# A one-core graph attention layer: the part up to the end of the first group laid out anew

## The reference

```python
h = jnp.maximum(_layernorm(x, axis=-1), 0.0)        # x: 4096 x 256
# the attention layer, on h:
h = h @ W.T
src = h @ a1
dst = h @ a2
e = jax.nn.leaky_relu(src[:, None] + dst[None, :], negative_slope=0.2)
e = jnp.where(adj == 0, -9e15, e)                   # adj: 4096 x 4096 int32
out = x + jax.nn.softmax(e, axis=1) @ h
```

## Time and profile before

| | us |
|---|---|
| median of 3 runs | 390.15 |
| lowest, highest | 389.91, 390.94 |
| profiled execution, its own time | 390.14 |
| its span | 388.6 |
| TensorE busy | 380.4 (98%) |
| VectorE busy | 366.8 (94%) |
| ScalarE busy | 196.7 (51%) |
| GpSimd busy | 43.6 (11%) |

### The profile page before, as it was taken

How to read it: one execution, slowest core, us unless ns; L and a number is a source line. 1 busy time by engine, 2 the same in 40 slices (tenths; PEclk the granted TensorE clock), 3 DMA queues, 4 the chain that set the end, 5 groups by cost and what they waited for, 6 DMA issues and landing times.

```text
span 388.6 us, 9271 instructions
## 1 busy us (share of the span) xinstructions
PE 380.4 (98%) x3368; PEld 330.2 (85%) x3368; DVE 366.8 (94%) x478; ACT 196.7 (51%) x282; POOL 43.6 (11%) x73
## 2 busy tenths in 40 slices
PE   6999899999999999999999999999999999999996
PEld 6788588888888888888888888888888888888885
DVE  4999999999999999999999799999988999999965
ACT  5899956553345643444445543444445543444430
POOL 3898002000000001110000001200000011100000
PEclk9999999999999999999999999999999999999999
DMA  8920176776559567776666567766665567766403
GB/s 255 371 79 3 43 246 222 267 232 231 171 175 292 182 216 218 244 232 220 221 221 205 183 216 231 240 221 220 215 205 179 167 217 239 229 231 215 162 2 108
DMA packets 26112, 77.95 MB, mean 201 GB/s; under 512 B 2916, under 2 KB 8552, under 8 KB 26088
## 3 DMA queue, kind: packets, MB, share of 16 engines
q1 hardware_dynamic: 24528, 74.20, 59.0%
q0 software_dynamic: 1280, 3.16, 2.2%
q10 hardware_dynamic: 280, 0.26, 0.3%
HBM read 73.40 MB, written 4.21 MB: 200 GB/s over the span
## 4 chain that ended last, share of the span: by engine, by line
PE 89%; DVE 4%; POOL 2%; ACT 1%; DMA 1%; issue 1%; ACTq 0%; DVEq 0%; POOLq 0%
PE ps L1280 87%; DMA w_f<-w_t 1%; POOL hn_sb L392 1%; DVE v_sb L767 1%; DVE hnt_lo L754 1%; PE ps L1218 1%; PE ps L1230 0%; ACT c_row L495 0%; DVE rows_sb L1130 0%; PE ps L1237 0%; PE ps L1234 0%; DVE hn_sb L762 0%; ACT hn_sb L474 0%; POOL v_sb L397 0%; ACT h_sb L467 0%
## 5 line engine op out<-in xcount | busy, mean ns | idle before, releaser
L1280 PE MATMUL ps<-v_sb,p_hi 128*128 (+2 forms) x2048 | 253.5, 272 | 1.4 <-ACT p_hi L505 1.4
L515 ACT ACTIVATE p_hi<-p_sb,gp 128x1024 f16<-128x1024 f32 x126 | 144.4, 1149 | 167.7 <-DVE p_sb L795 138.8
L1280 PEld LDWEIGHTS ps<-v_sb,p_hi 128*128 128x128 f16 x2048 | 198.3, 97 | 30.0 <-ACT p_hi L505 1.5
L802 DVE SCALAR_TENSOR_TENSOR p_lo<-p_sb,gp,p_hi 128x1024 f16<-128x1024 f32 x126 | 160.5, 1277 | 9.0 <-ACT p_hi L515 8.8
L795 DVE SCALAR_TENSOR_TENSOR p_sb<-c_row,gp,adj_sb 128x1024 f32<-128x1024 uint32 (+1 forms) x126 | 160.2, 1276 | 0.0
L1280 PE MATMUL ps<-v_sb,p_lo 128*128 (+1 forms) x1024 | 142.4, 273 | 0.0
L1280 PEld LDWEIGHTS ps<-v_sb,p_lo 128*128 128x128 f16 x1024 | 99.6, 97 | 13.5 <-DVE p_lo L788 0.3
L451 POOL DMA_DIRECT2D out<-rows_sb x24 | 13.0, 544 | 260.7 <-DVE rows_sb L1097 260.7
L392 POOL TENSOR_SCALAR hn_sb<-x_sb,moments,rstd 128x256 f32<-128x256 f32 x17 | 21.1, 1247 | 8.0 <-DVE rstd L744 8.0
L1218 PE MATMUL ps<-ident,hn_sb 128*128 128x128 f32 x64 | 12.8, 291 | 2.0 <-ACT hn_sb L474 1.5
L467 ACT ACTIVATE h_sb<-ps 128x258 f32<-128x258 f32 x32 | 12.2, 383 | 3.0 <-PE ps L1237 2.7
(11 more groups left out here) (96 smaller groups left out, 112.1 us busy)
## 6 DMA issues: line engine op xcount, KB each, us to landing
adj_sb<-adj_t SPq DMA_DIRECT2D x128, 512.0 KB, 4.8
x_sb<-x SPq DMA_DIRECT2D x7, 512.0 KB, 8.9
out<-rows_sb POOLq DMA_DIRECT2D x24, 128.0 KB, 4.5
c_row<-c_flat SPq DMA_DIRECT2D x3, 512.0 KB, 5.1
out<-rows_sb SPq DMA_DIRECT2D x8, 128.0 KB, 1.7
x_sb<-x SPq DMA_DIRECT2D x2, 256.0 KB, 4.3
w_nat<-w SPq DMA_DIRECT2D x1, 256.0 KB, 2.9
w_f<-w_t ACTq DMA_DIRECT2D x1, 256.0 KB, 5.2
```

Source lines behind the costliest of these rows:

```text
L515: nc.scalar.activation(p_hi[:, u % R, :], p_sb[:, u % R, :], ACT.Copy, scale=p_scale[:, bass.ds(t, 1)])\
L802: nc.vector.scalar_tensor_tensor(out=p_lo[:, u % R, :], in0=p_sb[:, u % R, :], scalar=p_scale[:, bass.ds(t, 1)], in1=p_hi[:, u % R, :], op ...
L1280: return nc.tensor.matmul(ps[:, k, 0:width], part[:, u % R, k * P:(k + 1) * P], v_sb[:, bass.ds(t, 1), v, 0:width], start=start, stop=stop ...
```

## The change

1. `w_f` is loaded on SyncE's queue, behind the first chunk of `x`, and no longer on ScalarE's.
2. Tiles 4 to 7 are one batch of statistics: nine batches in place of ten. VectorE normalises no tile any more (before 20, 25, 30); ScalarE has 14 (before 12), GpSimd 18 (before 17). `value_hi` falls to other engines for some tiles.
3. All turned tiles lie in one ring of RT = 8; `first_hi` and `first_lo` are gone.
4. `spread_s` with its twelve products and the copies `w1_hi`, `w1_lo` are gone. In their place `turn_s` turns the column s of each of tiles 0 to 7 from `h_sb`, broadcast to 128 columns: eight fp32 transposes of 128 columns, all behind `spread_d`. The exponent's scale for it is another column of `exp_scale`.
5. `spread_d` reads the last four tiles from the ring, one projection earlier; the turn of `d_up` is a step of its own, `turn_d`, into bank 1.
6. TensorE's order is a written list; `project` is cut in three (`project_hi`, `project_w_lo`, `project_lo`). One more product of `ones` stands behind the four of `w_nat`.
7. The lists of the other three engines are written anew. Before `d_up` VectorE has `value_lo` of tiles 0 to 9 (before 0 to 12), before the first `weights_part` 0 to 11 (before 0 to 14); GpSimd's five scale instructions stand behind its last `normalise`. In the first group VectorE waits for `p_lo_ready` of four tiles back ahead of every `edge_weights` from tile 4 on, before only ahead of some.

```diff
-    TURN_AHEAD = ((0, 1), (3, 2), (SOON, 3))
-    SPREAD_AFTER = {9: (0, 0), 11: (0, 1), 30: (1, 0), 31: (1, 1)}
+    BUSY_START, BUSY_SUMS, BUSY_SPLIT = 5, 1, 1
-    BATCHES = [(a, a + 2) for a in range(0, 2 * XB, 2)] + [(a, a + XB) for a in range(2 * XB, T, XB)]
+    BATCHES = [(0, 2), (2, 4), (4, 8), (8, 12), (12, 16), (16, 20), (20, 24), (24, 28), (28, 32)]
+    RT = 8
...
             for m, (t0, t1) in enumerate(X_CHUNKS):
                 sp.dma_start(x_sb[:, t0:t1, :], x_v[:, t0:t1, :]).then_inc(x_loaded[m], 16)
+                if m == 0:
+                    sp.dma_start(w_f[:, :, 0:F], w_tv).then_inc(w_t_loaded, 16)
...
-            act.dma_start(w_f[:, :, 0:F], w_tv).then_inc(w_t_loaded, 16)
...
-            def spread_s(m, c):
-
-                part = slice(m * CW, (m + 1) * CW)
-                last_chunk = c == KC - 1
-                nc.tensor.matmul(ps[:, bank_s + m, :], w1_hi[:, c, :], first_hi[:, c, part], start=(c == 0), stop=False)
-                nc.tensor.matmul(ps[:, bank_s + m, :], w1_lo[:, c, :], first_hi[:, c, part], start=False, stop=False)
-                last = nc.tensor.matmul(ps[:, bank_s + m, :], w1_hi[:, c, :], first_lo[:, c, part],
-                                        start=False, stop=last_chunk)
+            def turn_s(t):
+                pe.wait_ge(*kept(t))
+                last = nc.tensor.transpose(ps[:, bank_s + t // CT, t % CT * P:(t % CT + 1) * P],
+                                           h_sb[:, t, F:F + 1].to_broadcast([P, P]), ident[:])
+                if t % CT == CT - 1:
+                    last.then_inc(s_spread, 1)
...
+            def turn_d():
+                pe.wait_ge(d_part_ready, 1)
+                pe.wait_ge(hnt_lo_ready, LAST_IN_BANK_D_TURNED + 1)
+                nc.tensor.transpose(ps[:, banks_t[-1], 0:P], d_up[:, 0:1].to_broadcast([P, P]), ident[:]).then_inc(d_turned, 1)
```

More of the change, by code:

```diff
@@ L543, in _ @@
             split_hn_hi(2)
+            normalise(4)
+            split_hn_hi(3)
             keep_h(1)
+            keep_h(2)
+            split_hn_hi(4)
+            normalise(6)
             std_of(3)
[L546 to L550, removed]
             split_hn_hi(5)
-            std_of(4)
             keep_h(3)
@@ new lines, in _ @@
+            project_hi(0)
+            project_w_lo(0)
+            project_lo(0)
+            project_hi(1)
+            turn(2)
+            project_w_lo(1)
+            project_lo(1)
+            turn(3)
+            project_hi(2)
+            project_w_lo(2)
+            project_lo(2)
+            turn(4)
+            turn(5)
+            project_hi(3)
+            project_w_lo(3)
+            project_lo(3)
+            project_hi(4)
+            project_w_lo(4)
+            turn(6)
+            project_lo(4)
@@ new lines, in _ @@
+            turn(7)
+            project_hi(5)
+            project_w_lo(5)
+            project_lo(5)
+            project_hi(6)
+            project_w_lo(6)
+            project_lo(6)
+            turn(8)
+            project_hi(7)
+            project_w_lo(7)
+            turn(9)
+            project_lo(7)
+            turn(10)
+            project_hi(8)
+            project_w_lo(8)
+            project_lo(8)
+            project_hi(9)
+            project_w_lo(9)
+            project_lo(9)
@@ new lines, in _ @@
+            turn(11)
+            project_hi(10)
+            project_w_lo(10)
+            project_lo(10)
+            turn(12)
+            turn(13)
+            project_hi(11)
+            project_w_lo(11)
+            project_lo(11)
+            project_hi(12)
+            project_w_lo(12)
+            turn(14)
+            project_lo(12)
+            turn(15)
+            project_hi(13)
+            project_w_lo(13)
+            project_lo(13)
+            project_hi(14)
+            project_w_lo(14)
@@ new lines, in _ @@
+            project_lo(14)
+            turn(16)
+            project_hi(15)
+            project_w_lo(15)
+            project_lo(15)
+            turn(17)
+            project_hi(16)
+            project_w_lo(16)
+            project_lo(16)
+            turn(18)
+            project_hi(17)
+            turn(19)
+            project_w_lo(17)
+            project_lo(17)
+            project_hi(18)
+            project_w_lo(18)
+            project_lo(18)
+            turn(20)
+            project_hi(19)
@@ new lines, in _ @@
+            project_hi(24)
+            turn(26)
+            project_w_lo(24)
+            turn(27)
+            project_lo(24)
+            project_hi(25)
+            project_w_lo(25)
+            turn(28)
+            project_lo(25)
+            turn(29)
+            project_hi(26)
+            turn(30)
+            project_w_lo(26)
+            project_lo(26)
+            turn(31)
+            project_hi(27)
+            project_w_lo(27)
+            project_lo(27)
+            spread_d()
```

507 lines of the change are left out of this document (269 added, 238 removed).

## The result

The changed kernel takes 387.69 us (median of 4 runs, 387.32 to 388.21), the kernel before 390.24 (389.91 to 390.94, 4 runs). The ratio is 0.9936, with a 95% interval of 0.9922 to 0.9951: 2.5 us faster. The forecast was 386.9 within 385.4 to 389.1. The profiled execution took 388.21 with a span of 386.5, the longest of the four.

The account below looks back on a forecast made before the run. TensorE's unbroken 336.22 us of products was taken to bound the kernel, gaining only by starting earlier, behind a front bound by no one engine. 390.14 - 3.3 (front) + 0 + 0.1 (first group) = 386.9 us, range 385.4 to 389.1.

Parts of the forecast that it names:

- D: Start of the products for d (`spread_d`), where the front was cut: forecast at 36.4, 3.3 us earlier than 39.72.
- The start: Before turn 0: `w_f` lands sooner, so `w_hi` at 6.5 and turn 0 at 7.75, 0.5 us earlier; bounds 0 and 0.8.
- The low clock: TensorE from turn 0 on: 3.3 us at 1.2 GHz and not 2.4, counted as 1.65 us lost.
- TensorE's 34.9: The front: TensorE reaches D at 34.9 with no waits, from 7.75 + 25.5 of work + 1.65 for the clock.
- The waits: The front: D taken as VectorE's no-wait 35.5 plus half of its 1.6 us of waits; TensorE had 2.3 before.
- From D to the first group: Between D and the long piece of products: first product at D + 5.6, net 0, bounds -0.4 and +0.5.
- The first group: VectorE's three more `value_lo` there take 1.0 of 1.16 us of cover, leaving 0.15; cost 0.1, up to 0.5.
- all waits stay: Rival for the front: VectorE's and TensorE's waits of before remain, D 37.2, 387.7 us; chance 0.23 shared with rival 3.
- ScalarE's added `normalise` are waited out: Rival for the front: TensorE waits 6.6 us in all for them, D 41.5, time 392.0 us; chance 0.04.
- The collision on the ports: Front: each of ten `value_lo` waits half a GpSimd `normalise`, 6 us on VectorE, time 392.0 us; chance 0.01.
- rival 3: First group: VectorE at least 1 us later than counted, TensorE waits at the last tile, 387.9 us; chance 0.23, shared.
- rival 4: Front runs as planned, waits under 0.5 and full clock sooner: D 35.0 to 35.4, 385.5 to 385.9 us; chance 0.15.

Follow-up runs that it names:

- b_wt_sp: The kernel before with only the load of `w_f` moved to SyncE's queue behind the first chunk of `x`: 390.19 us against 389.97 in its session.
- a_wt_act: The changed kernel with the load of `w_f` back on ScalarE's queue: 387.48 us, ratio 0.9934 to the kernel before.
- a_group3: The changed kernel with three more 256-column subtractions, read by nobody, on VectorE in the first group: 388.35 us, ratio 0.9951 to the kernel before.
- b_turn_s: The kernel before with the twelve wide products for s and GpSimd's two copies replaced by eight turns of kept columns: 390.47 us against 390.12.

## Why the prediction was right, and where it was off

The sum was 390.14 - 3.3 at D + 0.1 behind it. The profile has -2.60 at D and +0.67 behind it. The median of 387.69 would stand for a D of 36.6 (an estimate: less the 351.05 behind D). So the number for D was close, by terms that were off in both directions, and 0.6 behind D was missing.

**The start.** `w_hi` 6.52 for 6.5, turn 0 7.79 for 7.75: right in this profile. Over the ten with this order of loads turn 0 came between 7.73 and 8.64, so it is also luck. The sum let the 0.5 us count in full; `b_wt_sp` and `a_wt_act` show that the part is worth nothing in the median.

**The low clock.** This term was mis-sized: 1.65 us, as if the 3.3 us from turn 0 on were fixed. In the profile it was 6.2 us at half speed, 3.1 lost. It is not fixed: the same front had 3.3 to 6.2 us. With 1.5 more, TensorE's 34.9 becomes 36.4, and D was 37.12, with waits of 0.7. The step that failed is taking one execution's moment as the program's.

**The waits.** I took VectorE's 35.5 and half of its waits for D = 36.4. The order was wrong: in the changed kernel the chain is TensorE alone up to D, with waits of 0.7 for the 2.3 before, and at the earliest full clock of this front (11.2) D was 35.77, again with TensorE's 34.9 and such waits. That VectorE's sum gave nearly the same number is luck; no run shows VectorE at its 35.5. GpSimd's last `normalise` ended at 35.4 and not near 33, still ahead of the turn of tile 31; it had waited for `rstd` for 3.4 us in all, not 2, and lost 0.47 us in that last one (1.69 for 1.22).

**From D to the first group.** Net 0 was forecast. The fifth tile (its first products at 53.94, before 56.39) stands 16.82 behind D, before 16.67: 0.15 lost. The first product came at D + 6.03, 0.4 later than I put it, since ScalarE waited 0.30 for the turns of s.

**The first group.** A cover of 0.15 was forecast, and a distance of 0.16 was there: from the fifth tile to the last TensorE took 71.53 us in both kernels, so nothing was lost, for a forecast of 0.1. But `a_group3` shows that the 0.16 is no slack. The view of waits has one of 0.2 for L790 on a weight load in this group, which did not hold up the products.

**The turn to the second group.** At the last tile of the first group the gain is 2.45; at the end of the last product 2.18 (380.95 for 383.13). The 0.27 between was lost right behind the first group, where the sum had no term. ScalarE copies the finished rows and TensorE's next sixteen products need those banks. Before:

```profile
129.05 2.29 ACT L696 ACTIVATE rows_sb<-ps 128x257 f32<-128x257 f32 x8
130.57 1.93 PE L1280 MATMUL ps<-v_sb,p_hi 128*128 128x257 f16 x16
132.34 1.04 PE L1280 MATMUL ps<-v_sb,p_lo 128*128 128x257 f16 x8
```

and after:

```profile
127.60 2.29 ACT L691 ACTIVATE rows_sb<-ps 128x257 f32<-128x257 f32 x8
128.12 2.21 PE L1409 MATMUL ps<-v_sb,p_hi 128*128 128x257 f16 x16
129.38 0.11 PEld L1409 LDWEIGHTS ps<-v_sb,p_hi 128*128 128x128 f16 x2 [0.16 <-ACT rows_sb L691]
130.17 1.04 PE L1409 MATMUL ps<-v_sb,p_lo 128*128 128x257 f16 x8
```

The sixteen products take 2.05 for 1.77, and the copies begin 2.13 behind the first product of the last tile, before 1.13. The changed kernel's waits have a row for it that the kernel before has not:

```profile
PEld ps L1409 <- ACT rows_sb L691: 0.8, 5, 0.2
```

VectorE's edge weights for the next group start 0.25 ahead of the last tile's first product (125.22), before 1.24 (126.68), and ScalarE's `p_hi` and copies follow them. So the us of cover that VectorE gave up in the first group is the us by which the copies come later. This is a reading of the rows; it was not tested. The last 0.2 of the 0.67 stand behind the last product and were not located.

**The rivals.** That all waits stay (387.7) gave the right number by the wrong way: TensorE's waits went from 2.3 to 0.7, and the clock took their place. That ScalarE's added `normalise` are waited out did not happen: in the front TensorE waited 0.37 and 0.41, both ahead of projection 0. The collision on the ports did not happen as priced either: two `value_lo` took 0.74 us at the start of that `normalise` of 1.69 and a third 0.41 at its end, so GpSimd lost 0.47 in all beside its neighbours, and VectorE nothing. The first group did not become VectorE's (rival 3), but with nothing to spare. A D of 35.0 to 35.4 (rival 4) stands in no profile.

```profile
33.62 0.74 DVE L755 TENSOR_TENSOR v_sb<-h_sb,v_sb 128x256 f16<-128x256 f32 x2
```

By the rule of the Trainium skill (SBUF — State Buffer, "Who interferes with whom") one of the two is blocked for the other's whole instruction. The trace does not bear that out: VectorE was not held for GpSimd's 1.22 us, and GpSimd lost less than the three `value_lo` of 0.34 each that stood beside it.

## What to carry to other kernels

Sum the work of every engine up to one point that all later work hangs on, and price each edit there: work taken from TensorE was worth nothing in a front where another list came last, and most of its time once the lists were rewritten. Sum behind the point too: an engine that gives up its cover is late for what comes next, even where nobody waits for it yet. One profile gives one landing of a load and one moment of the full clock. Both are spreads; take them from several profiles, and compare D with D only from a common step on, here projection 3.

## What the runs showed of the hardware that was not expected

- The clock of TensorE rose at 11.2, 11.9, 12.6, 13.2, 14.0 and 14.2 us in six executions of the same start, after turn 0 at 7.8 to 8.6. The view of the granted clock showed 1.00 for these stretches all the same; the distance between starts (0.43 or 0.22 us for a pair of 258 columns) is what shows it.
- Products of ones in its idle gap did not bring it forward in the kernel before: 11.8 without and 11.7 with them, although TensorE was shown busy from 4.0 us on. In the changed kernel two executions with filled gaps had 12.2 and 9.9, which is too few to tell.
- In one execution of `b_turn_s` it fell back to 1.2 GHz for some 3.4 us (granted clock 0.50 from 46 to 48, 0.65 from 48 to 50) behind two gaps of 0.9 us, and the long stretch behind was 1.5 us longer than its products account for (338.58 for 336.22 and eight products of 0.11).
- GpSimd's `normalise` of 256 columns took 1.69 us and not 1.22 with three `value_lo` of VectorE beside it, which kept their 0.34 each.
